# First stage of a graph network layer: x transposed loaded whole, bucket counts interleaved with the chunks of h

## The chip, the cores and the metric

The kernel runs on one core of one Trainium2 chip. The metric is device time in microseconds, the median of several runs. The core has TensorE (PE), VectorE (DVE), ScalarE (ACT), GpSimd (POOL) and SyncE (SP), which run on their own and wait for each other through semaphores, and 16 DMA engines that move what SP, ACT and POOL issue. SP's transfers go through one queue (q1 in the profile), ACT's through another (q10).

## What is computed

```python
h = x @ W_in2f                                        # x: 6250 x 128
Wij = ssp(f_ij @ W_filt1 + b_filt1) @ W_filt2 + b_filt2   # 200000 edges, 20 features
Wij = Wij * rcut_ij[:, None]
x_ij = h[idx_j] * Wij                                 # idx_j = dst, sorted
agg = segment_sum(x_ij, idx_i, num_segments=6250)     # idx_i = src, random
out = ssp(agg @ W_out1 + b_out1) @ W_out2 + b_out2
return layernorm(x + out)
```

`ssp` is softplus less log 2.

## The kernel before

Every engine has its program written out by hand; nothing is reordered by a scheduler. There are three parts.

**The first stage** (the subject here) computes h in 13 chunks of 512 nodes, the last of 256. For chunk n, PE multiplies the transposed x with `w_in` into `pre_psum[n % 2]` (`node_features`), ACT copies the high bf16 part to `h_out` (`h_hi`), DVE takes the rest (`h_left`), ACT its bf16 part (`h_mid`), DVE the last part (`h_lo`), and SP stores the three parts to `h_parts` in HBM (`store_h`). In front of each high part ACT also issues DMAs that fill four tables in HBM with zeros, 20 of 640 KB in all (`zero`). Both x and `h_out` have two buffers: SP loads x chunk by chunk (`load_x_t`), and ACT waits until the store two chunks back has landed. Chunks 0 and 1 stand alone, 2 to 11 in a loop of two per turn.

The first stage also prepares indices. DVE reduces `dst_g` (102 partitions of 2048 values) to window bases that go to HBM and come back (`window_base`, `base_all`), and casts `dst_g` and `src_g` to 16 bits, which SP stores (`dst`, `src`, semaphore `edges16_stored`) and reads back as broadcasts (`dst_b`, `src_b`). One fourth of the edge groups is routed by a table of 14 buckets of nodes: after chunk 1, `place_routed` on DVE marks which edge lies in which bucket (`in_bucket`), PE counts with four matmuls per bucket (`count_in_buckets`), and DVE multiplies each count with its mark and adds it to `rank`. `judge_windows` then sets the flag `narrow`, on which all engines branch, and `make_biases` splits the biases.

**The main loop** takes 391 groups of 512 edges. Of the groups that aren't routed, POOL adds the rows to the tables with indirect DMAs of 128 rows each (`scatter`, line 729), 1115 in all. Its order on each engine is a fixed list (`unit`). **The last layers** read the tables and write the output.

SP and POOL run their queues in order too: a wait holds back every transfer issued behind it.

Of the kernel before, what the change touches and what calls it, by code (L numbers as in the profile page):

```python
# [61 lines left out]
META_HOTS, META_STEPS = 20, 49  # L62
# [223 lines left out]
def build(nc, t):  # L286
    with ExitStack() as ctx:
# [75 lines left out]
        acc_t = sb("acc_t", [P, NODE_ROWS], F32)  # L363
# [16 lines left out]
        x_t = at(37632, "x_t", [P, 2, CHUNK], F32)  # L380
        h_out = at(41728, "h_out", [P, 2, 4, 3, DIM], BF16)
        h_rest = at(47872, "h_rest", [P, 2, 4, DIM], F32)
        bucket = at(51968, "bucket", [P, ROUTES * TILES], F32)
        local = at(53760, "local", [P, ROUTES * TILES], F32)
        src_r = at(55552, "src_r", [P, ROUTES * TILES], I32)
        in_bucket = at(58496, "in_bucket", [P, BUCKETS, ROUTES * TILES], BF16)
        rank = at(71040, "rank", [P, ROUTES * TILES], F32)
        rank_part = at(72832, "rank_part", [P, ROUTES * TILES], F32)
        bias_tmp = at(74880, "bias_tmp", [P, 2, 3, DIM], F32)
        bias_hi = at(77952, "bias_hi", [P, 2, 3, DIM], BF16)  # L390
        base_all = at(79488, "base_all", [P, SLOTS], F32)
        spread_row = at(81120, "spread_row", [1, SLOTS], F32)
# [30 lines left out]
        zeros_made, tables_zeroed = sem("zeros_made"), sem("tables_zeroed")  # L423
# [34 lines left out]
        meta_step, meta_mm, crowd_mm = sem("meta_step"), sem("meta_mm"), sem("crowd_mm")  # L458
# [28 lines left out]
        def run_chunks(eng, step, last):  # L487
            step((0, 0), CHUNK // P)
            step((0, 1), CHUNK // P)
            with eng.Fori(0, FULL_CHUNKS // 2 - 1) as j:  # L490
                step((j, 2), CHUNK // P)
                step((j, 3), CHUNK // P)
            step((0, FULL_CHUNKS), last // P)
# [281 lines left out]
        def _(act):  # L775
# [14 lines left out]
            for fifth in range(2):  # L790
                zero(0, fifth)
# [1365 lines left out]
```

## Time and profile before

| | us |
|---|---|
| median of 3 runs (lowest, highest) | 2372.86 (2367.43, 2375.89) |
| the profiled execution | 2375.85 |
| its span, from the first to the last instruction | 2373.8 |
| busy in the span: PE / DVE / ACT / POOL | 2162.8 / 1676.7 / 1642.3 / 1828.8 |
| last chunk of h split by DVE | 111.1 |
| first matmul of the main loop | 111.9 |
| first scatter / last scatter ends its chain | 128.3 / 2276.4 |

The span is read as three lengths: up to the first scatter, the scatters, and what is behind them. Matmul and DMA times are those of this one execution. TensorE runs at one of two clocks, and a row of windows gives the mean that was granted as a share of the full one.

### The profile page before, as it was taken

The page shows a single profiled execution, that of the slowest core. Times are in us where ns is not written, and L with a number is a line of the kernel's source. Part 1 is how long each engine was busy: PE and PEld are TensorE (multiplying, and loading weights), DVE is VectorE, ACT ScalarE, POOL GpSimd, SP SyncE. Part 2 cuts the span into 40 slices and gives each one's busy share as a digit, 9 for nine tenths or more (in the row PEclk, how much of TensorE's full clock was granted, in tenths as well). Part 3 has the DMA queues.
Part 4 walks back from the last instruction along what each step waited for, and adds up shares of the span by engine and source line. Part 5 has one row for each costly group of instructions (what it writes and reads, how often), then busy time and mean ns, then how long its engine had stood idle before and what let it go on. Part 6 is the DMA issues. An engine that isn't in the chain of part 4 may idle for free.

```text
span 2373.8 us, 60910 instructions
## 1 busy us (share of the span) xinstructions
PE 2162.8 (91%) x16558; PEld 1441.8 (61%) x16558; DVE 1676.7 (71%) x3915; ACT 1642.3 (69%) x3676; POOL 1828.8 (77%) x1148
## 2 busy tenths in 40 slices
PE   2488999999999999999999999999999999999947
PEld 1355666666656666666666666666666666666536
DVE  5466777777777777777776777777676768777627
ACT  0277777777777777777776877777776867777513
POOL 2068888888888888888888888888888888888831
PEclk8599999999999999999999999999999999999979
DMA  6676666666656666666666666666666656666555
GB/s 207 265 151 95 97 95 91 100 99 90 97 95 94 97 96 97 93 94 99 93 95 94 100 90 100 95 96 92 96 97 89 101 94 98 91 97 99 58 122 164
DMA packets 370946, 250.03 MB, mean 105 GB/s; under 512 B 88787, under 2 KB 350142, under 8 KB 370314
## 3 DMA queue, kind: packets, MB, share of 16 engines
q0 software_dynamic: 160560, 73.14, 32.6%
q1 hardware_dynamic: 199482, 155.27, 27.2%
q10 hardware_dynamic: 10476, 16.77, 1.9%
q8 instruction: 164, 2.69, 0.5%
q14 instruction: 264, 2.16, 0.4%
HBM read 149.90 MB, written 95.13 MB: 103 GB/s over the span
## 4 chain that ended last, share of the span: by engine, by line
DMA 44%; POOL 18%; PE 17%; issue 16%; DVE 3%; ACT 1%; POOLq 0%; SPq 0%; DVEq 0%; ACTq 0%
DMA table<-total,index 41%; POOL table L729 18%; PE unit_psum L1859 4%; PE unit_psum L1878 3%; PE both_psum L1815 2%; PE total_psum L1828 2%; PE pre_psum L1802 2%; DMA src_g<-in_src 1%; DMA h_parts<-h_out 1%; PE both_psum L2086 1%; PE both_psum L1840 1%; PE both_psum L1811 1%; PE both_psum L2084 0%; PE total_psum L2108 0%; PE pre_psum L2094 0%
## 5 line engine op out<-in xcount | busy, mean ns | idle before, releaser
L729 POOL DMA_INDIRECT table<-total,index x1115 | 1801.1, 1615 | 445.1 <-issue 244.6
L1859 PE MATMUL unit_psum<-moving,route_hot 128*128 128x386 bf16 x3136 | 608.1, 331 | 40.3 <-ACT ring L909 34.6
L879 ACT ACTIVATE h_dst<-both_psum,cols 128x128 f32<-128x128 f32 x1564 | 448.8, 385 | 104.2 <-PE both_psum L1840 104.2
L1878 PE MATMUL unit_psum<-scat_hot,ring 64*128 64x448 bf16 x4704 | 478.7, 351 | 9.6 <-DVE scat_hot L1416 6.1
L1859 PEld LDWEIGHTS unit_psum<-moving,route_hot 128*128 128x128 bf16 x3136 | 295.8, 99 | 267.5 <-ACT ring L909 103.6
L909 ACT ACTIVATE ring<-unit_psum 128x386 bf16<-128x386 f32 x784 | 373.2, 508 | 120.5 <-PE unit_psum L1859 82.0
L1815 PEld LDWEIGHTS both_psum<-w_f,hidden 128*128 128x128 f32 x3128 | 418.0, 194 | 18.3
L1815 PE MATMUL both_psum<-w_f,hidden 128*128 128x128 f32 x3128 | 418.8, 277 | 0.0
L1878 PEld LDWEIGHTS unit_psum<-scat_hot,ring 64*128 64x128 bf16 x4704 | 216.0, 94 | 216.9 <-DVE acc_t L1432 7.4
L1828 PE MATMUL total_psum<-message,same 128*128 128x129 f32 x2232 | 310.1, 281 | 4.0 <-DVE message L1344 2.4
L843 ACT ACTIVATE soft<-pre_psum 128x1024 f32<-128x1024 f32 x196 | 201.8, 1030 | 160.9 <-PE pre_psum L1802 159.8
L1828 PEld LDWEIGHTS total_psum<-message,same 128*128 128x128 f32 x2232 | 277.6, 192 | 36.5 <-issue 26.1
L862 ACT ACTIVATE total<-total_psum 128x516 f32<-128x516 f32 x279 | 171.2, 614 | 146.5 <-DMA table<-total,index 137.4
L1392 DVE TENSOR_SCALAR route_hot<-node_iota,cols 128x896 bf16<-128x896 uint16 x448 | 193.0, 477 | 98.8 <-PE unit_psum L1859 98.0
L1416 DVE TENSOR_SCALAR scat_hot<-node_iota,slot_node 128x448 bf16<-128x448 uint16 x784 | 255.9, 353 | 4.3 <-PE unit_psum L1878 2.5
L1297 DVE TENSOR_TENSOR same<-src_b,cols 128x512 f32<-128x512 uint16 x279 | 191.3, 686 | 93.7 <-PE total_psum L1828 92.7
L1318 DVE SCALAR_TENSOR_TENSOR hidden<-pre_psum,soft 128x1024 f32<-128x1024 f32 x196 | 238.9, 1219 | 21.0 <-ACT soft L855 19.6
L1344 DVE TENSOR_TENSOR message<-both_psum,h_dst 128x512 f32<-128x512 f32 x279 | 191.1, 685 | 84.3 <-ACT h_dst L879 37.0
L1802 PE MATMUL pre_psum<-f_t,w_f 32*128 32x512 f32 x784 | 224.7, 649 | 15.2 <-DVE hidden L1318 10.8
L849 ACT ACTIVATE soft<-soft 128x1024 f32<-128x1024 f32 x196 | 212.6, 1085 | 0.0
L855 ACT ACTIVATE soft<-soft 128x1024 f32<-128x1024 f32 x196 | 210.6, 1075 | 1.1
L1308 DVE TENSOR_SCALAR pick<-dst_b,cols 128x512 bf16<-128x512 uint16 x391 | 149.7, 383 | 85.5 <-PE both_psum L1840 65.9
(116 smaller groups left out, 1635.6 us busy)
## 6 DMA issues: line engine op xcount, KB each, us to landing
dst_b<-dst SPq DMA_DIRECT2D x391, 128.0 KB
src_b<-src SPq DMA_DIRECT2D x279, 128.0 KB, 4.3
f_t<-in_f_t SPq DMA_DIRECT2D x98, 256.0 KB
table<-total,index POOLq DMA_INDIRECT x1115
table<-zeros ACTq DMA_DIRECT2D x20, 640.0 KB, 5.6
window<-h_parts SPq DMA_DIRECT2D x391, 32.0 KB
parts<-table SPq DMA_DIRECT2D x48, 256.0 KB, 4.0
h_parts<-h_out SPq DMA_DIRECT2D x12, 384.0 KB, 5.4
```

The source lines that it names most:

```text
L729: pool.indirect_dma_start(tables[table], bass.IndirectOffsetOnAxis(index[:, i, k:k + 1], 0), total[:, i, k, 0:DIM], None, compute_op=ALU.a ...
L849: act.activation(soft[:, :, :], soft[:, :, :], ACT.Exp, scale=-1.0).then_inc(exp_done, 1)
L855: act.activation(soft[:, :, :], soft[:, :, :], ACT.Ln, bias=1.0).then_inc(soft_done, 1)
L879: last = act.activation(h_dst[:, b, d], source, ACT.Copy, scale=cols[:, g[1] // HALF % 2, weight:weight + 1])
L909: act.activation(ring[:, r[1] % RING, k, :], unit_psum[:, k % 2, 0:MOVING], ACT.Copy).then_inc(ring_done, 1)
L1318: dve.scalar_tensor_tensor(hidden[:, first:first + 2, :], pre_psum[:, :, :], 0.0, soft[:, :, :], ALU.max, ALU.add).then_inc(hidden_done, 1)
L1416: dve.tensor_scalar(scat_hot[:, r[1] % RING, :], node_iota[:, 0:BUCKET], slot_node[:, r[1] % RING, k:k + 1], None, ALU.is_equal).then_inc( ...
L1802: last = pe.matmul(pre_psum[:, a, :], w_f1[row:row + BAND, :], f_t[row:row + BAND, quad[1] % 2, :], start=True, stop=True)
L1815: last = pe.matmul(filter_psum[:, d], hidden[:, g[1] % QUAD, k * P:(k + 1) * P], w_f2[:, :], start=False, stop=(k == TILES - 1))
L1828: last = pe.matmul(total_psum[:, k // 2, d], same[:, b, k, :], message[:, b, k, :], start=True, stop=True)
L1859: last = pe.matmul(unit_psum[:, k % 2, 0:MOVING], route_hot[:, tile, k * P:(k + 1) * P], moving[:, tile, :], start=(tile == 0), stop=(tile ...
L1878: last = pe.matmul(unit_psum[:, strip, 0:BUCKET], ring[rows, r[1] % RING, slot_tile(m), part * DIM:(part + 1) * DIM], scat_hot[rows, r[1] ...
```

## The change

- **x**: `x_t` lies whole in the space of `acc_t` (the accumulator that POOL clears later). SP loads it in three parts (4, 4 and 5 chunks, `X_PARTS`), the first right behind `dst_g`, the others behind `src_g`; `src_i` and `weight_c` now come last.
- **h**: four buffers of `h_out` (`H_BUFFERS`); ACT waits for the store four chunks back. The loop is unrolled. SP issues no loads of x between the stores, and its first loads for the main loop (`load_first_edges`: features, `dst_b`, `src_b`) stand behind the store of chunk 6, not ahead of the stores.
- **counts**: DVE does `make_order` and the marks (`place_routed`) ahead of chunk 0. PE counts bucket n behind the matmuls of chunk n (bucket 13 last), and DVE multiplies with the mark between its two halves of chunk n (`take_ranks`), into two buffers of `rank_part`.
- **ranks**: the 13 additions are done by POOL, which does the cast of `src_g` first. POOL clears `acc_t` behind them, since x lies there.
- **tail**: `place_slots`, `judge_windows` and `make_biases` stand behind the last chunk; the bias matmuls too. PE's first matmul needs only `w_in`, and not all constants.
- **zeros**: ACT issues them between its two copies of a chunk, one table after another (`ZEROS_BY_CHUNK`: 2, 2, 2, 2, 1, 2, 1, 2, 1, 2, 1, 1, 1), and the first scatter of each table waits for that table alone.

```diff
+H_BUFFERS = 4
+X_PARTS = (0, 4, 8, 13)
+ZEROS_BY_CHUNK = (0, 2, 4, 6, 8, 9, 11, 12, 14, 15, 17, 18, 19, 20)
...
+            load_x_t(0)
             sp.dma_start(src_r[:, :], t["src_routed"]).then_inc(src_routed_loaded, 16)
-            sp.dma_start(src_i[:, :], t["src_cols"]).then_inc(src_cols_loaded, 16)
-            load_x_t((0, 0), CHUNK // P)
-            load_x_t((0, 1), CHUNK // P)
-            sp.dma_start(weight_c[:, :], t["weight_cols"]).then_inc(cols_loaded, 16)
             sp.dma_start(src_g[:, :, :], t["src"].rearrange("(p g e) -> p g e", p=QUADS, e=GROUP)
                          ).then_inc(src_loaded, 16)
+            load_x_t(1)
+            load_x_t(2)
+            sp.dma_start(src_i[:, :], t["src_cols"]).then_inc(src_cols_loaded, 16)
+            sp.dma_start(weight_c[:, :], t["weight_cols"]).then_inc(cols_loaded, 16)
...
+            def store_chunk(c, tiles):
+                store_h(c, tiles)
+                if is_at(c, CHUNKS // 2):
+                    load_first_edges()
+
+            run_chunks(store_chunk)
...
+            pool.wait_ge(src_loaded, 16)
+            pool.tensor_copy(src_g16[:, :], src_g[:, :, :].rearrange("p g e -> p (g e)")).then_inc(src16_made, 1)
             pool.wait_ge(src_cols_loaded, 16)
             pool.tensor_copy(edge_cols[:, :, 0:WEIGHT_COL], by_half(src_i[:, :])).then_inc(cols_made, 1)
             pool.wait_ge(cols_loaded, 16)
             pool.tensor_copy(edge_cols[:, :, WEIGHT_COL:WINDOW_COL], by_half(weight_c[:, :])).then_inc(cols_made, 1)
+
+            for b in range(1, BUCKETS):
+                pool.wait_ge(rank_taken, b + 1)
+                if b > 1:
+                    pool.wait_ge(rank_summed, b - 1)
+                pool.tensor_tensor(rank[:, :], rank[:, :], rank_part[:, b % 2, :], ALU.add).then_inc(rank_summed, 1)
+            pool.wait_ge(h_mm, CHUNKS)
             pool.memset(acc_t[:, :], 0.0).then_inc(acc_zeroed, 1)
...
             def split_h(c, tiles):
-                b = c[1] % 2
...
+                b, out = c[1] % 2, c[1] % H_BUFFERS
                 act.wait_ge(h_mm, after_chunk(c))
-                previous(act, h_stored[b], c, landed_chunk)
...
+                if c[1] >= H_BUFFERS:
+                    act.wait_ge(h_stored[out], 16 * (c[1] // H_BUFFERS))
...
+                for n in range(ZEROS_BY_CHUNK[c[1]], min(ZEROS_BY_CHUNK[c[1] + 1], FIFTHS * TABLES)):
+                    zero(n // FIFTHS, n % FIFTHS)
                 act.wait_ge(h_left, after_chunk(c))
...
+            def take_ranks(b):
+
+                dve.wait_ge(count_mm, b + 1)
+                dve.wait_ge(bucket_hot, BUCKETS)
+                if b >= 3:
+                    dve.wait_ge(rank_summed, b - 2)
+                part = rank[:, :] if b == 0 else rank_part[:, b % 2, :]
+                dve.tensor_tensor(part, unit_psum[:, b % 2, 0:ROUTES * TILES], in_bucket[:, b, :], ALU.mult
+                                  ).then_inc(rank_taken, 1)
...
+            make_order()
+            place_routed()
+            run_chunks(split_h)
+            for b in range(CHUNKS, BUCKETS):
+                take_ranks(b)
+            place_slots()
+            judge_windows()
+            make_biases()
```

On VectorE, behind chunk 1 of h, the program before has its marks, then 14 products and 13 additions in a row (the first of them here; `h_rest` and `h_out` are the two halves of a chunk):

```order
L1276 TENSOR_TENSOR h_out<-h_rest,h_out 128x4x128 [waits h_left,h_mid]
L1202 TENSOR_SCALAR rank_part<-src_r 128x448 [waits consts_made,src_routed_loaded]
L1205 TENSOR_SCALAR rank<-rank_part 128x448 [waits meta_step]
L1207 TENSOR_SCALAR bucket<-rank 128x448 [waits meta_step]
...
L1228 TENSOR_TENSOR rank<-unit_psum,in_bucket 128x448 [waits meta_step,meta_mm]
L1228 TENSOR_TENSOR rank_part<-unit_psum,in_bucket 128x448 [waits meta_step,meta_mm]
L1233 TENSOR_TENSOR rank<-rank,rank_part 128x448 [waits meta_step]
```

With the change the same engine has the marks ahead of chunk 0, and one product inside each chunk (here the end of the marks and chunks 0 and 3):

```order
L1225 CAST local_parts<-local 128x448 [waits local_step]
L1227 TENSOR_TENSOR local_parts<-local,local_parts 128x448 [waits local_step]
L1278 TENSOR_TENSOR h_rest<-pre_psum,h_out 128x512 [waits h_hi]
L1237 TENSOR_TENSOR rank<-unit_psum,in_bucket 128x448 [waits bucket_hot,count_mm]
L1284 TENSOR_TENSOR h_out<-h_rest,h_out 128x4x128 [waits h_left,h_mid]
...
L1278 TENSOR_TENSOR h_rest<-pre_psum,h_out 128x512 [waits h_lo,h_mid,h_hi]
L1237 TENSOR_TENSOR rank_part<-unit_psum,in_bucket 128x448 [waits rank_summed,bucket_hot,count_mm]
L1284 TENSOR_TENSOR h_out<-h_rest,h_out 128x4x128 [waits h_left,h_mid]
```

The additions are gone from VectorE, and each product from the fourth on waits for one of GpSimd's additions (`rank_summed`).

SyncE's queue with the change, from its start to the flag (`x_t` is x transposed, `h_parts` the stores):

```order
L544 DMA dst_g<-in_dst 102x2048
L535 DMA x_t<-in_x_t 128x2048
L547 DMA src_r<-in_src_routed 128x448
L548 DMA src_g<-in_src 102x2048
L535 DMA x_t<-in_x_t 128x2048
L535 DMA x_t<-in_x_t 128x2304
L552 DMA src_i<-in_src_cols 128x1632
L553 DMA weight_c<-in_weight_cols 128x1632
L556 DMA window_base<-dst_low 102x4 [waits spans_made]
L557 DMA window_spread<-dst_spread 102x4
L560 DMA dst<-dst_g_56 102x2048 [waits dst16_made]
L562 DMA src<-src_g_57 102x2048 [waits src16_made]
```

```order
L564 DMA base_all<-window_base 128x408 [waits spans_stored]
L565 DMA spread_row<-window_spread 1x408
L539 DMA h_parts<-h_out 128x1536 [waits h_lo] x7
L571 DMA f_t<-in_f_t 128x512 x2
L576 DMA dst_b<-dst 128x512 [waits edges16_stored]
...
L539 DMA h_parts<-h_out 128x1536 [waits h_lo] x5
L539 DMA h_parts<-h_out 128x768 [waits h_lo]
```

All of x, `src_i` and `weight_c` now stand ahead of the small store of the windows, and every store of h stands behind the wait for that store to land (`spans_stored`). Before, only 512 KB of x and the same columns stood there, and the loop of stores came last too.

## Rows read from the trace of the kernel before

**Rows 1.** Windows by stage: busy us (instructions) of each engine, TensorE clock, DMA share.

```profile
core 0: us, PE busy (x) PEld busy (x) DVE busy (x) ACT busy (x) POOL busy (x), PEclk, DMA share, GB/s
...
49.00:72.00 23.00, 12.16 (x55) 7.08 (x54) 20.92 (x48) 0.72 (x2) 0.00 (x0) 0.84 0.25 79
72.00:110.00 38.00, 19.00 (x68) 16.39 (x68) 13.33 (x20) 11.90 (x20) 0.00 (x0) 0.50 0.98 381
...
128.30:2276.40 2148.10, 2037.95 (x15884) 1346.33 (x15883) 1560.05 (x3605) 1585.99 (x3568) 1801.14 (x1115) 0.99 0.63 95
```

**Rows 2.** Timeline from 110 to 130 us: start, us, engine, line.

```profile
110.69 0.43 DVE L1276 TENSOR_TENSOR h_out<-h_rest,h_out 128x256 bf16<-128x256 f32 x1 [0.48 <-ACT h_out L808]
...
111.90 2.08 PE L1802 MATMUL pre_psum<-f_t,w_f 32*128 32x512 f32 x4 [3.91 <-issue]
...
128.34 1.73 POOL L729 DMA_INDIRECT table<-total,index  x1 [100.16 <-DVE index L1363]
```

**Rows 3.** DMA answer for 22 to 26 us, packets and busy share by queue.

```profile
DMA packets 98, 0.48 MB, mean 120 GB/s; under 512 B 33, under 2 KB 33, under 8 KB 50
...
q1 hardware_dynamic: 48, 0.39, 31.2%
```

**Rows 4.** DMA answer for 76 to 110 us, packets and landing times.

```profile
DMA packets 4092, 13.37 MB, mean 393 GB/s; under 512 B 448, under 2 KB 576, under 8 KB 4092
...
table<-zeros ACTq DMA_DIRECT2D x11, 640.0 KB, 4.6
h_parts<-h_out SPq DMA_DIRECT2D x8, 384.0 KB, 5.3
```

**Rows 5.** DMA issues from 0 to 130 us, KB of each, two sizes.

```profile
dst_g<-in_dst SPq DMA_DIRECT2D x1, 816.0 KB
...
dst<-dst_g SPq DMA_DIRECT2D x1, 408.0 KB
```

**Rows 6.** Timeline of the first 44 us, VectorE and SyncE's queue.

```profile
14.80 2.29 DVE L1144 TENSOR_REDUCE dst_low<-dst_g 102x4 f32<-102x2048 int32 x1 [14.80 <-DMA dst_g<-in_dst]
...
29.69 1.23 DVE L1151 CAST src_g<-src_g 102x2048 uint16<-102x2048 int32 x1 [9.00 <-DMA src_g<-in_src]
...
34.06 0.35 SPq L555 DMA_DIRECT2D base_all<-window_base  x1
...
35.57 0.39 DVE L1202 TENSOR_SCALAR rank_part<-src_r 128x448 f32<-128x448 int32 x1
...
42.18 0.66 DVE L1220 TENSOR_TENSOR local_parts<-local,local_parts 128x448 bf16<-128x448 f32 x1
...
43.64 0.33 SPq L567 DMA_DIRECT2D dst_b<-dst  x1
```

**Rows 7.** Groups of instructions from 43 to 72 us, counts and ranks.

```profile
L1767 PE MATMUL unit_psum<-in_bucket,ones_bias 128*128 128x336 bf16 (+2 forms) x42 | 10.4, 367 | 0.0
...
L1233 DVE TENSOR_TENSOR rank<-rank,rank_part 128x448 f32<-128x448 f32 x13 | 8.1, 624 | 0.4
L1765 PE MATMUL unit_psum<-in_bucket,earlier 128*128 128x448 bf16 x14 | 6.5, 466 | 15.7 <-DVE local_parts L1220 11.3 <-DVE rank_part L1228 4.3
```

**Rows 8.** Groups of instructions from 72 to 111.5 us, chunks of h.

```profile
L1780 PE MATMUL pre_psum<-w_in,x_t 128*128 128x128 f32 x68 | 19.1, 460 | 19.7 <-DMA x_t<-in_x_t 17.0 <-DVE h_rest L1271 2.7
...
L1276 DVE TENSOR_TENSOR h_out<-h_rest,h_out 128x512 bf16<-128x512 f32 (+1 forms) x11 | 7.3, 668 | 7.4 <-ACT h_out L808 7.4
...
L804 ACT ACTIVATE h_out<-pre_psum 128x512 bf16<-128x512 f32 (+1 forms) x10 | 5.8, 576 | 18.2 <-DMA h_parts<-h_out 18.2
```

**Rows 9.** Groups by form, GpSimd's only addition.

```profile
L769 POOL TENSOR_TENSOR half_sum<-parts 128x512 f32<-128x512 f32 x12 | 15.2, 1265 | 58.6 <-DMA parts<-table 58.6
```

**Rows 10.** Timeline of VectorE behind the last rank addition, and biases.

```profile
62.67 0.62 DVE L1233 TENSOR_TENSOR rank<-rank,rank_part 128x448 f32<-128x448 f32 x1
...
70.21 0.91 DVE L1194 COPY bias_o<-bias_hi 1x512 bf16<-1x512 bf16 x3
```

**Rows 11.** Timeline at 35 us, one issue on ScalarE's queue.

```profile
34.97 1.58 ACTq L783 DMA_DIRECT2D table<-zeros  x1
```

More of the change, by code:

```diff
@@ L485, in run_units, with run_chunks @@
             rest()
[L487 to L493, printed above, removed]
+        def run_chunks(step):
+            for n in range(CHUNKS):
+                step((0, n), (LAST_H if n == CHUNKS - 1 else CHUNK) // P)
         def run_last_layers(eng, step):
@@ L506, in previous, with h_landed @@
                 eng.wait_ge(s, count(plus(c, -n)))
+        def h_landed(eng):
+            for b in range(H_BUFFERS):
+                eng.wait_ge(h_stored[b], 16 * len(range(b, CHUNKS, H_BUFFERS)))
         def done_with(eng, s, g, kind=every, n=0):
@@ L624, in step_narrow @@
                 if is_at(g, 1):
-                    for k in range(2):
-                        sp.wait_ge(h_stored[k], 16 * (FULL_CHUNKS // 2 + (k == 0)))
+                    h_landed(sp)
                     load_window((0, 0))
@@ L758, in _ @@
                 pool.wait_ge(cols_made, 2)
-                for b in range(2):
-                    pool.wait_ge(h_stored[b], 16 * (FULL_CHUNKS // 2 + (b == 0)))
+                h_landed(pool)
                 run_groups(pool, step_general)
@@ new lines, in make_biases, with count_in_bucket @@
+            def make_biases():
+                pe.wait_ge(consts_loaded, 16 * 7)
+                pe.matmul(total_psum[:, 0, 0:DIM], minus_ln2[:, :], w_f2[:, :], start=True, stop=True)
+                pe.matmul(total_psum[:, 0, DIM:2 * DIM], minus_ln2[:, :], w_o2[:, :], start=True, stop=True
+                          ).then_inc(bias_mm, 1)
+            def count_in_bucket(b):
+                counts = unit_psum[:, b % 2, 0:ROUTES * TILES].rearrange("p (g k) -> p g k", k=TILES)
+                here = in_bucket[:, b, :].rearrange("p (g k) -> p g k", k=TILES)
+                pe.wait_ge(bucket_hot, b + 1)
+                if b >= 2:
+                    pe.wait_ge(rank_taken, b - 1)
+                pe.matmul(counts, earlier[:, :], here, start=True, stop=False)
+                for a in range(1, TILES):
+                    last = pe.matmul(counts[:, :, a:TILES], ones_bias[:, :], here[:, :, 0:TILES - a],
+                                     start=False, stop=(a == TILES - 1))
+                last.then_inc(count_mm, 1)
```

237 lines of the change are left out of this document (98 added, 139 removed).

## The prediction

> **What bounds the kernel now.** I read the windows by stage first, to see which part of the span the change can touch. From 128.3 to 2276.4 us GpSimd issues all 1115 scatters, 2148.1/1115 = 1.93 us each, with TensorE busy 2038 of the 2148 us [rows 1]. The diff leaves the instructions of this part as they are, and each waits only for others of the same part, so it keeps its length and moves as a whole. What counts is the start. The timeline gives it: VectorE ends the last chunk at 110.69 + 0.43 = 111.1, the first matmul of the main loop begins at 111.9, the first scatter at 128.34 [rows 2], 16.4 us after that matmul. The work between these two is unchanged as well.
>
> So the question is when the first stage ends. Its windows show two halves that don't overlap. From 49 to 72 us VectorE is busy 20.9 of 23 us with counts, flag and biases, and the DMA engines 25%. From 72 to 110 us the DMA engines are busy 98% at 381 GB/s and VectorE 13.3 of 38 us [rows 1]. There ScalarE waited 18.2 us for stores of h to land [rows 8], TensorE 17.0 us for x. The first half wastes the DMA engines, the second is bound by them: laying them over each other is what this change can gain, and DMA time is what limits it.
>
> **How fast the DMA engines are.** From 76 to 110 us they moved 393 GB/s [rows 4]; over 16 engines that is 24.6 GB/s, 24 KB (of 1024) per us and engine. They don't share evenly: between 22 and 26 us, when only `src_g` was left on SP's queue, that queue kept 31% of 16 = 5 engines busy [rows 3]. `src_g` has 102 partitions, 6 x 17, so I take it that such a transfer lies on six engines, 816/6 = 136 KB on each [rows 5]. The trace doesn't name the six. The Trainium skill does (DMA: Bandwidth & Descriptors, "Why a DMA increments its semaphore by 16 and not by 1"): the largest count up to 16 that divides the slowest dimension, and always the lowest-numbered engines; the 31% agrees. By it all four such transfers pile up on the same six; spread over all 16, the transfers of the sum below would be done 170/24 = 7 us earlier.
>
> On one of the six, behind `dst_g`, there are on SP's queue: x 200, `src_r` 14, `src_g` 136, `src_i` and `weight_c` 51 each, `dst` and `src` 408/6 = 68 each, `base_all` 13, the stores of h 12 x 24 + 12 = 300, and the first edges 2 x 16 + 7 x 8 = 88: 989 KB. ScalarE's queue adds 20 x 40 = 800 KB of zeros. At 24 KB/us these 1789 KB take 74.5 us.
>
> **Part by part.**
> *Start.* `dst_g` is first on SP as before, and the constants are the same, so it lands at 14.8 [rows 6]. Its two reductions and the cast end at 20.7. VectorE then no longer waits for `src_g` (it did until 29.69), but does `make_order` (0.9 us) and the marks, which took 35.57 to 42.84, 7.3 us [rows 6]: chunk 0 begins on VectorE at 28.9. TensorE and ScalarE have their part of it by 20, since the first quarter of x lands 64/24 = 2.7 us behind `dst_g`.
>
> *Engines per chunk.* TensorE: 19.1/8.5 = 2.25 us for h [rows 8] and (10.4 + 6.5)/14 = 1.21 us for a count [rows 7], both mostly at its lower clock (0.50 granted in that window), 3.5 us. VectorE: 0.67 + 0.62 + 0.67 and handoffs, 2.2 us [rows 7, 8]. GpSimd: its addition of 512 columns took 1.265 us [rows 9], so 1.11 us for 448; hidden under the chunk. ScalarE: two copies of 0.6 us and the zeros' issue, up to 1.58 us each [rows 11], 2.8 to 4.4 us. None of this is the bound if the next step holds.
>
> *The stall.* Chunk 4 waits for store 0 to land. Store 0 is issued only when the small store of the windows has landed, which stands behind all of x and both columns. Ahead of its landing are on the six engines x 200, 14, 136, 102, 136, 13 and its own 24: 625 KB, and the zeros of chunks 0 to 3, 8 x 40 = 320 KB. 945/24 = 39.4 us from 14.8 gives 54.2. The small store itself, rows of 16 bytes, held SP from `src_g`'s landing at 29.69 to 34.06 [rows 6], 4.4 us; half of that overlaps with zeros, so 2 more: 56. The way of counting, tried on before: from 34.06 the two 16-bit stores (136 KB) and three tables of zeros (120) in front of `dst_b`'s issue at 43.64 [rows 6] take 10.7 us; the trace has 9.6. The other waits are shorter: GpSimd starts its additions behind `weight_c` (about 43), and VectorE's product 3 waits for one of them, but both end before 56.
>
> *From 56 on* the two queues share: 12 KB/us for SP. Chunk 11 needs store 7, behind stores 1 to 7 (168 KB) and the first edges (88): 256/12 = 21 us, 77. TensorE alone would bring chunk 11 at 56 + 6 x 3.5 = 77 too, being two chunks ahead. Chunk 12 follows at 79, and VectorE ends it at T = 81. The last store lands at 86, all zeros by about 90: both before they are needed.
>
> *The tail.* What lay under nothing before lies under nothing now: product 13 (0.62), GpSimd's addition (1.11), handoffs 0.2, then the same work as from 63.3 to 71.1, 7.8 us [rows 10]; then TensorE reads the flag and starts, 1.6 us (0.8 behind VectorE's last instruction before [rows 2], and that one it didn't wait for). 11.3 us in all: first matmul at 92.3 instead of 111.9. Clearing `acc_t` on GpSimd (5.3 us) moves behind the additions and fits under the 16.4 us.
>
> *Zeros by table.* The first scatter at 108.7 finds all zeros landed, as it did before: 0.
>
> Sum: -19.6 us. Span 2373.8 - 19.6 = 2354.2; the profiled execution took 2375.85, 3 us above the median of 2372.86, which becomes 2353.
>
> *A rule that speaks against it.* No row has VectorE and GpSimd adding from SBUF at once. The Trainium skill (SBUF — State Buffer, "Who interferes with whom") says that a VectorE instruction with two SBUF inputs and a GpSimd one that reads SBUF exclude each other. By it each chunk's second half could wait one addition: 3.3 us of VectorE per chunk, below TensorE's 3.5, and the total would be about 2354.
>
> **Rivals.**
> *A. The engines are the bound, the DMA engines are not* (15%). If the zeros take less of the six engines than half, store 0 lands before chunk 4 asks. Then 11 chunks at TensorE's 3.5 us from 29.6 and the last split end at 70, first matmul 81.5, total 2342. For it: a 64 KB share that lands in 3 us when its queue has the engines. Against: 98% busy with fewer zeros per us than now.
> *B. The old pace from chunk 4 on* (14%). From 72 to 110 a chunk took about 4.2 us; 56 + 9 x 4.2 = 94, first matmul 105, total 2366. For it: stores took 5.3 us to land [rows 4], and queue depth might count, not bytes. Against: x is no longer in that queue.
> *C. The shift is lost in the main loop* (6%): total 2370 to 2373. GpSimd is idle 347 us in it [rows 1], so a lost start could be made up there; but TensorE, at 95%, starts later too.
> *D. Slower* (5%). The small store in front of all stores of h: its 16-byte rows alternate with zeros on the same engines. If it lands so late that store 0 comes after 75.6 (then T passes 100.6 and the first matmul 111.9), the kernel is slower; at 81 by 5 us, 2378. It took 4.4 us before with at most one table beside it, and would need some 20.
>
> **How the numbers follow.** The likeliest case, DMA-bound with the stall at 56, has 60%; its own range is 2346 to 2361, by store 0 at 50 to 62. The range for 8 in 10 runs from A to B, 2341 to 2367. 0.3% is 7 us, about what this measurement can tell, as its own runs lie 8 us apart. Faster by more than that: the likeliest, A and half of B, 0.83; within it: the rest of B and C, 0.12; slower: 0.05.
>
> **What would show it.** First matmul of the main loop at 90 to 95, first scatter 16 behind. ScalarE idle some 10 us ahead of chunk 4's high part, released by a store of `h_parts`; SP's queue held at `base_all` to 43 or later. DMA share above 0.8 from 30 to 86. Main loop unchanged at 2148. Wrong: chunk 4 before 50 (A), chunks 8 to 12 apart by 4 us (B), a longer main loop (C), `base_all` after 60 (D).

## The result, and the profile after

| | before | after |
|---|---|---|
| median of 4 (lowest, highest) | 2374.27 (2367.43, 2375.89) | 2409.68 (2407.33, 2415.37) |
| ratio, 95% interval | | 1.0152 (1.0135 to 1.017) |
| span of the profiled execution | 2373.8 | 2413.3 |
| first matmul of the main loop | 111.9 | 104.46 |
| first scatter | 128.34 | 121.72 |
| from the first scatter to the end of the last one's chain | 2148.1 | 2189.0 |
| behind that | 97.4 | 102.6 |

The change made the kernel 1.5% slower. The start moved forward as forecast in sign (6.6 us, not 19.6), the main loop became 40.9 us longer, and 5.2 us were lost behind it: -6.6 + 40.9 + 5.2 = 39.5 us, the difference of the spans. Of the 5.2 no cause was found, and it may be none: the part behind the last scatter took between 96 and 103 us in kernels of both kinds (96.5 in `a_pad62` below, 101.7 in `b_pad34`, which has the old first stage).

**The first stage after.** Windows of the changed kernel, columns as in [rows 1]; the last row is the part from the first scatter on.

```profile
0.00:30.00 30.00, 8.81 (x33) 6.92 (x34) 16.32 (x33) 3.00 (x4) 5.55 (x18) 0.99 0.94 252
30.00:56.40 26.40, 9.13 (x40) 7.18 (x38) 6.03 (x10) 2.87 (x6) 6.71 (x5) 0.63 0.70 277
56.40:84.90 28.50, 17.80 (x80) 14.68 (x80) 19.17 (x21) 8.03 (x15) 7.92 (x7) 0.80 0.99 375
84.90:104.50 19.60, 2.38 (x12) 1.53 (x12) 16.46 (x35) 2.22 (x5) 8.80 (x4) 0.50 0.31 122
121.70:2310.70 2189.00, 2051.70 (x15883) 1356.50 (x15880) 1559.84 (x3605) 1586.55 (x3567) 1786.52 (x1115) 0.97 0.61 94
```

Overlap came about: the DMA engines are busy 94, 70 and 99% up to 84.9, where before they were at 25% from 49 to 72 [rows 1]. Then come 19.6 us at 31%. The timeline shows what lies at the seams (L815 is the start of a chunk on ScalarE, here chunks 4 and 11; L1284 the last part of chunk 11).

```profile
46.23 0.36 SPq L564 DMA_DIRECT2D base_all<-window_base  x1
...
56.39 0.60 ACT L815 ACTIVATE h_out<-pre_psum 128x512 bf16<-128x512 f32 x1 [21.06 <-DMA h_parts<-h_out]
...
66.19 2.49 SPq L571 DMA_DIRECT2D f_t<-in_f_t  x2
...
78.19 11.92 SPq L539 DMA_DIRECT2D h_parts<-h_out  x6
...
84.89 0.60 ACT L815 ACTIVATE h_out<-pre_psum 128x512 bf16<-128x512 f32 x1 [9.17 <-DMA h_parts<-h_out]
...
86.82 1.13 POOL L726 TENSOR_TENSOR rank<-rank,rank_part 128x448 f32<-128x448 f32 x1 [10.02 <-DVE rank_part L1237]
...
86.91 1.59 DVE L1284 TENSOR_TENSOR h_out<-h_rest,h_out 128x512 bf16<-128x512 f32 x1 [0.17 <-ACT h_out L821]
...
91.94 5.32 POOL L728 MEMSET acc_t<- 128x6272 f32 x1
...
93.47 4.01 DVE L1260 TENSOR_SCALAR edge_cols<-base_all,row_node 128x408 f32<-128x408 f32 x1
...
104.46 2.08 PE L1817 MATMUL pre_psum<-f_t,w_f 32*128 32x512 f32 x4 [11.38 <-issue]
...
121.72 1.73 POOL L747 DMA_INDIRECT table<-total,index  x1 [24.45 <-issue]
```

Chunk 4 starts on ScalarE at 56.39, behind a wait of 21 us for store 0 (forecast: 56, behind some 10 us). From 66.19 to 78.19 SyncE issues the first edges, 12 us for nine transfers; the stores of h stand behind them, and ScalarE waits 9.2 us for store 7 ahead of chunk 11: 84.89, forecast 77. The last part of h is done at 89.75, forecast 81. Beside GpSimd's addition (86.82) the last part of a chunk (L1284) takes 1.59 us. The clearing of `acc_t` at 91.94 lies over `judge_windows`, whose 128x408 operation takes 4.01 us. First matmul 104.46, forecast 92.3.

**The main loop after.** TensorE's waits from 128 to 2300 us (line, what it waited for, us in total, times, longest), changed kernel and then the one before:

```profile
PE both_psum L1830 <- issue: 48.8, 13, 4.6
PE both_psum L1826 <- issue: 29.3, 13, 2.5
PE unit_psum L1874 <- ACT ring L922: 20.6, 25, 3.1
```

```profile
PE unit_psum L1859 <- ACT ring L909: 34.6, 41, 3.3
...
PE both_psum L1811 <- issue: 33.1, 13, 3.8
```

The loop has 13 turns. Each kernel loses 2.3 to 2.5 us per turn in "issue", a wait for nothing that the profile shows, ahead of the first matmul of a turn. The changed one has a second such wait per turn, in the midst of the matmuls of L1830: 48.8 us. The turn at 636 us, after and before:

```profile
635.61 0.39 PE L1826 MATMUL both_psum<-bias_f,ones_bias 96*128 96x512 bf16 x1 [2.04 <-issue]
635.84 0.72 PE L1830 MATMUL both_psum<-w_f,hidden 128*128 128x128 f32 x5
640.87 1.01 PE L1830 MATMUL both_psum<-w_f,hidden 128*128 128x128 f32 x3 [4.31 <-issue]
641.67 2.78 PE L1874 MATMUL unit_psum<-moving,route_hot 128*128 128x386 bf16 x8
```

```profile
636.08 0.39 PE L1811 MATMUL both_psum<-bias_f,ones_bias 96*128 96x512 bf16 x1 [2.27 <-issue]
636.31 1.06 PE L1815 MATMUL both_psum<-w_f,hidden 128*128 128x128 f32 x8
637.20 1.48 PE L1859 MATMUL unit_psum<-moving,route_hot 128*128 128x386 bf16 x8
```

Eight matmuls of one line run as one before; now three of them start 4.31 us later. And what follows runs slower, 2.78 us for the eight matmuls that took 1.48. The windows of the changed kernel from the gap on show the clock:

```profile
635.70:640.80 5.10, 0.86 (x6) 0.64 (x6) 0.00 (x0) 2.38 (x6) 4.19 (x4) 0.60 0.79 139
640.80:650.00 9.20, 9.13 (x52) 6.46 (x54) 4.39 (x8) 4.34 (x11) 7.79 (x5) 0.67 0.51 70
```

TensorE did 0.86 us of work in 5.1, and the granted clock falls to 0.60 and 0.67, a mix of the 1.2 and the 2.4 GHz level; the kernel before has 1.00 there. So the balance of the loop is +48.8 for the second stall, -3.8 at the first, -14.0 at the waits for the ring (ScalarE can catch up meanwhile), +13.8 of busy time (2051.7 against [rows 1]). That is 44.8 us; by difference the waits not listed are some 4 us shorter, which leaves the 40.9.

### The profile page after: what moved, and what is told of

The parts are those of the page before. It is cut to its first block, busy times and chain, and to the rows that moved or that the text cites. A ratio compares the mean times of both kernels' runs of the same rounds, so it can differ in the third digit from the quotient of the medians.

```text
span 2413.3 us, 60781 instructions
## 1 busy us (share of the span) xinstructions
PE 2177.6 (90%) x16558; PEld 1455.5 (60%) x16558; DVE 1678.5 (70%) x3901; ACT 1642.3 (68%) x3676; POOL 1831.1 (76%) x1162
## 4 chain that ended last, share of the span: by engine, by line
PE 36%; DMA 31%; issue 15%; POOL 11%; DVE 3%; ACT 2%; SPq 1%; POOLq 0%; DVEq 0%; ACTq 0%
DMA table<-total,index 28%; POOL table L747 10%; PE unit_psum L1874 9%; PE unit_psum L1893 8%; PE both_psum L1830 6%; PE total_psum L1843 5%; PE pre_psum L1817 4%; PE both_psum L1855 2%; PE both_psum L1826 1%; DMA window_spread<-dst_spread 1%; ACT ring L922 1%; PE both_psum L2101 1%; DMA h_parts<-h_out 1%; ACT h_dst L892 1%; DMA parts<-table 1%
## 5 line engine op out<-in xcount | busy, mean ns | idle before, releaser
L1874 PE MATMUL unit_psum<-moving,route_hot 128*128 128x386 bf16 x3136 | 617.4, 335 | 22.7 <-ACT ring L922 20.6
L1830 PE MATMUL both_psum<-w_f,hidden 128*128 128x128 f32 x3128 | 422.9, 278 | 48.8 <-issue 48.8
L1830 PEld LDWEIGHTS both_psum<-w_f,hidden 128*128 128x128 f32 x3128 | 418.6, 194 | 69.8 <-issue 51.5
L1843 PE MATMUL total_psum<-message,same 128*128 128x129 f32 x2232 | 315.0, 284 | 4.2 <-DVE message L1355 2.7
L1843 PEld LDWEIGHTS total_psum<-message,same 128*128 128x128 f32 x2232 | 282.8, 195 | 36.0 <-issue 24.6
L875 ACT ACTIVATE total<-total_psum 128x516 f32<-128x516 f32 x279 | 171.8, 616 | 112.3 <-DMA table<-total,index 99.8
L1817 PE MATMUL pre_psum<-f_t,w_f 32*128 32x512 f32 x784 | 224.7, 649 | 21.9 <-issue 11.4
```

The source lines that it names most:

```text
L1817: last = pe.matmul(pre_psum[:, a, :], w_f1[row:row + BAND, :], f_t[row:row + BAND, quad[1] % 2, :], start=True, stop=True)
L1830: last = pe.matmul(filter_psum[:, d], hidden[:, g[1] % QUAD, k * P:(k + 1) * P], w_f2[:, :], start=False, stop=(k == TILES - 1))
L1843: last = pe.matmul(total_psum[:, k // 2, d], same[:, b, k, :], message[:, b, k, :], start=True, stop=True)
L1874: last = pe.matmul(unit_psum[:, k % 2, 0:MOVING], route_hot[:, tile, k * P:(k + 1) * P], moving[:, tile, :], start=(tile == 0), stop=(tile ...
```

## The experiments

All times are medians of 4 to 10 runs. The ratios are against runs of the kernel before taken beside each kernel: their median was 2374.3 for the changed kernel, 2375.3 for `b_pad66` and the three that begin with a, 2374.4 for `b_pad34` and those with c, 2377.7 for those with d. "First matmul" and "scatters" (from the start of the first to the start of the last scatter) are of one profiled execution each, which lies up to 7.3 us from the median of its kernel. Positions count the instructions of TensorE's program as built (a bf16 matmul with its weight load is 2, a float32 one 4).

| kernel | loop starts at | median | ratio to before (95%) | first matmul | scatters |
|---|---|---|---|---|---|
| before | 3889 | 2374.3 | | 111.9 | 2144.6 |
| after | 4021 | 2409.7 | 1.0152 (1.0135, 1.0170) | 104.5 | 2185.6 |
| b_pad34 | 3956 | 2372.4 | 0.9996 (0.9979, 1.0012) | 109.3 | 2140.7 |
| b_pad66 | 4020 | 2412.8 | 1.0153 (1.0133, 1.0172) | 108.3 | 2183.4 |
| a_pad12 | 4045 | 2374.6 | 0.9995 (0.9981, 1.0008) | 104.9 | 2148.8 |
| a_pad62 | 4145 | 2371.4 | 0.9987 (0.9973, 1.0001) | 104.5 | 2140.2 |
| c_memset_late | 4145 | 2369.7 | 0.9981 (0.9965, 0.9998) | 106.0 | 2145.7 |
| a_pad62_dve | 4145 | 2364.0 | 0.9957 (0.9941, 0.9973) | 99.4 | 2148.9 |
| d_stores_first | 4145 | 2364.0 | 0.9948 (0.9927, 0.9969) | 99.8 | 2141.7 |
| d_biases | 4145 | 2360.8 | 0.9944 (0.9922, 0.9967) | 96.0 | 2142.7 |
| c_edges_last | 4145 | 2358.6 | 0.9929 (0.9908, 0.9950) | 89.8 | 2153.1 |
| c_zeros_late | 4145 | 2355.4 | 0.9928 (0.9907, 0.9950) | 90.7 | 2144.5 |
| d_all_edges6 | 4145 | 2352.5 | 0.9891 (0.9858, 0.9923) | 85.2 | 2146.0 |
| d_all | 4145 | 2349.2 | 0.9880 (0.9843, 0.9917) | 82.1 | 2143.4 |

### Where the loop lies in TensorE's program

The diff puts 132 instructions more ahead of TensorE's loop, by unrolling the chunks; the loop itself, 2211 instructions, is the same. Theory F: the second stall depends on where the loop starts. Rival: something that the new first stage leaves behind (table zeros, buffers, the order of queues) slows the loop. The edit is small matmuls into a corner of PSUM that isn't in use yet ahead of TensorE's first real one, 62 and 12 of them in the changed kernel, 66 in the kernel before:

```diff
+            pe.wait_ge(consts_made, CONSTS)
+            for _ in range(62):
+                pe.matmul(both_psum[0:1, 0, 0:1], ones_bias[:, 0:1], ones_bias[:, 0:1], start=True, stop=True)
             pe.wait_ge(w_in_loaded, 16)
-            pe.wait_ge(consts_made, CONSTS)
```

`a_pad62`, expected:

> The changed kernel with 62 one-element matmuls on TensorE ahead of its first real one (124 instructions with their weight loads), where it waits for x anyway. Theory F, place in the code: the change moved the start of TensorE's main loop by +132 instructions, so that a block of code ends about 14 instructions behind the loop's start and every turn waits 3.8 us for the next block; 124 more make the shift 256, a multiple of 128 and of 256, and the second stall (48.8 us over 13 turns at line 1830's matmuls) is gone: span about 2413 - 45 to 50 = 2363 to 2368, main loop 2140 to 2150, clock 0.99. Theory G, data traffic or the new places of buffers slow the loop: nothing changes, 2410 +- 5, main loop 2187.

`b_pad66`, expected:

> The kernel before with 66 one-element matmuls on TensorE (132 instructions) while it waits for its constants, nothing else changed: the loop starts within one instruction of where the changed kernel has it. F: a second stall of 3 to 4.5 us in each of 13 turns appears and the time is 2373 + 40 to 55 = 2413 to 2428, though the first stage is the old one. G: 2373 +- 5.

`a_pad12`, expected:

> The changed kernel with 12 such matmuls (24 instructions): the loop starts some 10 instructions behind the end of a block, with nearly a whole block ahead of it. F: as with 62, the second stall is gone, 2363 to 2368; if the distance mattered otherwise, the stall moves elsewhere in the turn. G: 2410.

Measured: 124 instructions more make the changed kernel 38 us faster, and 131 more make the kernel before 37 to 38 us slower. The medians lie 3 to 7 us above the 2363 to 2368 that was expected of `a_pad62` and `a_pad12`, and that of `b_pad66` just under its 2413 to 2428; theory G, with 2405 or more for the first two and 2378 or less for the third, is far off. TensorE's waits of `a_pad62`, then of `b_pad66`:

```profile
PE unit_psum L1876 <- ACT ring L922: 39.2, 46, 2.9
...
PE both_psum L1828 <- issue: 30.8, 13, 3.7
```

```profile
PE both_psum L1817 <- issue: 46.4, 13, 4.2
PE both_psum L1813 <- issue: 30.1, 13, 2.9
```

`a_pad62` has no second stall, `b_pad66` has it at the same matmuls as the changed kernel (L1817 is its L1830), with the old first stage. The rival is out. `a_pad12`, 24 instructions on, is free of it too (29.4 us at the first stall alone).

The stall falls behind the 14th instruction of a turn in the changed kernel (two of loop control, one bf16 matmul, five of the eight records of four float32 ones: 2 + 2 + 10) and behind the 16th in `b_pad66` (six of eight), that is, at 4035 to 4036 of the program in both. `a_pad12`, which starts past it, doesn't stall. So something ends there, and a turn that starts 14 or 16 instructions ahead of it stalls. How far ahead is enough? `b_pad34` starts 79 ahead:

> Kernel before with 34 one-element bf16 matmuls ahead of TensorE's first real one: its loop starts at instruction 3956 of its program (before: 3889, where a turn has one stall for code; 4020: two). If the second stall comes because the loop starts only some 14 instructions ahead of the end of a block of 256 that is fetched as one, 79 are enough: one stall per turn of 2.2 to 2.8 us, and the median within 0.3% of before, 2368 to 2380. Rival: what counts is the length of the code ahead (every added instruction slows), or the distance needed is over 79: a second stall per turn, median 2390 to 2415.

```profile
PE both_psum L1813 <- issue: 32.2, 13, 3.2
```

One stall per turn, 2372.4 us. The Trainium skill (Runtime: NRT & Kernel Launch, "Instruction fetch mechanics") says that an engine's code is fetched in 16 KiB blocks of 256 instructions, one after the other, and that a jump to a block outside the current window of two forces a fetch before the engine goes on. The trace agrees: the instruction queue q8 moves packets of 16.4 KB, and every kernel stalls once per turn, at the jump.

The packets also stand in the traces with their times (`--dma` with a narrow window). In the turn at 636 us one lands at 634.07, and the first matmul of the turn starts at 635.61; the next lands at 639.46, and the second stall ends at 640.87. So it is in all 13 turns of the changed kernel and of `b_pad66`: a packet lands 1.5 to 1.9 us ahead of the end of the first stall, and another 1.2 to 1.6 us ahead of the end of the second. Kernels without the second stall have two such packets as well. There the second lands 2.2 to 4.8 us after the turn's first matmul, and TensorE works meanwhile. So the next block arrives 2 to 5 us into the turn wherever the loop lies; with 14 to 16 instructions left in the first one the engine has run dry, with 79 it hasn't (0.7 us of such waits in all of `b_pad34`). Nothing in the trace names the engine that a packet of q8 belongs to; that these are TensorE's is inferred from their place, at 26 of 26 second stalls. The count alone doesn't tell the kernels apart (174 in the changed kernel, and 174 in `b_pad34`, which doesn't stall twice).

### GpSimd beside VectorE

In `a_pad62` the first stage still ends 12 us later than forecast. Part of it is the tail, 14.9 us there (14.7 in the changed kernel) from the last part of h to the first matmul instead of 11.3. `a_pad62_dve` gives the 13 rank additions back to VectorE, behind each product:

```diff
+                    dve.tensor_tensor(rank[:, :], rank[:, :], rank_part[:, b % 2, :], ALU.add).then_inc(rank_summed, 1)
```

> As with 62, and the 13 additions of ranks on VectorE again, right behind each product. Theory L: an addition on GpSimd and a VectorE instruction with two inputs in SBUF exclude each other (h_out took 1.60 instead of 0.69 us beside each addition). Undone, a chunk costs VectorE 2.0 + 0.65 instead of 2.9 us, and the tail loses GpSimd's addition but keeps one of 0.62: 1 to 3 us faster than with 62. Rival: VectorE doesn't set the pace of the chunks (the stores do), so equal to the run with 62 within 2 us.

```profile
73.49 5.33 POOL L723 MEMSET acc_t<- 128x6272 f32 x1 [32.74 <-PE pre_psum L1785]
...
84.36 0.60 ACT L810 ACTIVATE h_out<-pre_psum 128x512 bf16<-128x512 f32 x1 [11.30 <-DMA h_parts<-h_out]
...
92.00 0.40 DVE L1258 TENSOR_SCALAR edge_cols<-base_all,row_node 128x408 f32<-128x408 f32 x1
...
99.38 2.08 PE L1817 MATMUL pre_psum<-f_t,w_f 32*128 32x512 f32 x4 [7.77 <-issue]
```

VectorE does 0.63 us more per chunk, and a chunk goes from 2.9 us down to 2.4, since L1282 takes 0.69 us again and not 1.59. At the end of h that gives only 0.3 us (89.3 against 89.6), since store 7 holds chunk 11 as before. The rest, more than expected, came in the tail, 10.0 us: with no additions ahead of it, the clearing moves to 73.49 and the 128x408 operation takes 0.40 us instead of 4.01. First matmul 99.4, 5.1 us earlier; median 7.4 us lower. Is it the clearing? `c_memset_late` leaves the additions on GpSimd and clears behind the flag:

```diff
             pool.wait_ge(h_mm, CHUNKS)
-            pool.memset(acc_t[:, :], 0.0).then_inc(acc_zeroed, 1)
-
             pool.wait_ge(flag_made, 1)
+            pool.memset(acc_t[:, :], 0.0).then_inc(acc_zeroed, 1)
```

> Base: the changed kernel with 62 small matmuls ahead of TensorE's program (2371.4 us; rank additions on GpSimd; first matmul at 104.5). Only difference: GpSimd clears acc_t behind the flag and not ahead of it. Theory M (the clearing holds VectorE's operations while it runs: the 128x408 subtraction took 4.0 us beside it): that operation takes 0.4 us, the tail from the last part of h to the first matmul falls from 14.7 to 10 to 11.5 us, and the first matmul comes at 100 to 101.5; the wait then falls on VectorE's operations at the start of the main loop instead, of which one takes 3 us or more beside the clearing, so that the median falls by 0 to 3 us. Rival N (the 4.0 us are the late landing of base_all or a queue of SBUF writes): the operation stays at 4 us, the tail at 14 to 15.

```profile
93.82 0.40 DVE L1259 TENSOR_SCALAR edge_cols<-base_all,row_node 128x408 f32<-128x408 f32 x1
...
95.50 5.32 POOL L729 MEMSET acc_t<- 128x6272 f32 x1 [3.16 <-DVE narrow L1269]
...
95.84 5.13 DVE L1191 CAST bias_hi<-bias_tmp 128x256 bf16<-128x256 f32 x1
```

The 128x408 operation is free (0.40 us), and the cast of 128x256, 0.29 us by itself, starts 0.34 us after the clearing and ends with it: 5.13 us. The tail gained nothing (15.9 us), so half of the expectation failed (first matmul 106.0, not 100 to 101.5), and for the very reason that theory M names: the collision moved on to the next such instruction, ahead of the first matmul and not behind it. The landing of `base_all` (rival N) is out. The median, 1.6 us below that of `a_pad62`, is within the scatter of both.

Not every instruction is held by it. In `c_edges_last`, below, the clearing runs from 74.61 to 79.94 and L1282, which reads two operands of SBUF, takes 0.68 us in its midst. The Trainium skill (SBUF — State Buffer, "Who interferes with whom") has both: two SBUF inputs collide with a GpSimd instruction that reads SBUF, not with one that only writes; casts and `tensor_scalar`, in their fast modes, with either. Which mode an instruction took isn't in the trace, but the durations agree on each: the last part of a chunk beside an addition 1.59, beside the clearing 0.68; the scalar operation and the cast beside the clearing 4.01 and 5.13.

### What holds store 7

Theory S: SyncE's 12 us of issue. Theory T: the bandwidth, 99% busy from 56 to 85. Two edits on `a_pad62_dve`. `c_edges_last`:

```diff
-                if is_at(c, CHUNKS // 2):
+                if is_at(c, CHUNKS - 1):
                     load_first_edges()
```

> Base: the changed kernel with 62 small matmuls ahead of TensorE's program and the rank additions on VectorE (2364.0 us; chunk 11 of h waits 11.3 us for store 7, first matmul of the main loop at 99.4). Only difference: SyncE's 9 first loads for the main loop are issued behind the store of chunk 12, not behind that of chunk 6. Theory S (the 12 us in which SyncE issues them hold back store 7): ScalarE's wait ahead of chunk 11 ends at 73 to 77 instead of 84.4, the last part of h is done at 79 to 83, and first_edges then take some 4 us of issue and land by 90; the first matmul comes at 91 to 95 and the median falls by 4 to 8 us. Rival T (the transfer bandwidth is the bound there, 370 GB/s and 97% busy from 56 to 85): the waits stay within 2 us of 84.4 and the median within 2 us, or is later because the edges now land later.

`c_zeros_late`, one zero transfer per chunk and seven behind the last:

```diff
-ZEROS_BY_CHUNK = (0, 2, 4, 6, 8, 9, 11, 12, 14, 15, 17, 18, 19, 20)
+ZEROS_BY_CHUNK = (0, 1, 2, 3, 4, 5, 6, 7, 8, 9, 10, 11, 12, 13)
```

> Same base. Only difference: one zero transfer per chunk of h, and the 7 that are left (4.6 MB) behind the last chunk. Theory T (bandwidth bound from 56 to 85): ahead of chunk 11 there are 5 to 6 zeros fewer, 3.5 MB or some 9 us at 390 GB/s, so ScalarE's wait ends 6 to 9 us earlier and the first matmul comes at 91 to 94; the first edges issue faster too. The median falls by 3 to 8 us unless the last tables' zeros (now landing at about 105 to 110) hold a scatter. Theory S: SyncE's issue of the first edges stays at 10 to 12 us and store 7 as late, within 2 us.

`c_edges_last` (chunk 11 on ScalarE is the second row), then `c_zeros_late`:

```profile
74.61 5.33 POOL L723 MEMSET acc_t<- 128x6272 f32 x1 [32.69 <-PE pre_psum L1785]
...
74.76 0.60 ACT L810 ACTIVATE h_out<-pre_psum 128x512 bf16<-128x512 f32 x1 [0.71 <-DMA h_parts<-h_out]
...
77.19 0.68 DVE L1282 TENSOR_TENSOR h_out<-h_rest,h_out 128x512 bf16<-128x512 f32 x1
...
80.13 3.58 SPq L571 DMA_DIRECT2D f_t<-in_f_t  x2
...
89.44 0.35 DVE L1317 TENSOR_SCALAR pick<-dst_b,cols 128x512 bf16<-128x512 uint16 x1 [0.71 <-DMA dst_b<-dst]
```

```profile
60.53 1.46 SPq L571 DMA_DIRECT2D f_t<-in_f_t  x2
...
75.02 0.60 ACT L810 ACTIVATE h_out<-pre_psum 128x512 bf16<-128x512 f32 x1 [6.31 <-DMA h_parts<-h_out]
```

Both theories get their gain: chunk 11 starts 9.6 us earlier without the edges in front, 9.3 us earlier with fewer zeros beside them; the first matmuls, 89.8 and 90.7, came a little ahead of the expected 91. But the second gain is made of two: in `c_zeros_late` chunk 4 already starts at 52.23 and not 55.98, 3.8 us earlier, and ahead of chunk 11 6.3 us of the 11.3 remain. In `c_zeros_late` SyncE's issue of the edges takes 60.53 to 68.07, 7.5 us instead of 12, against theory S, which had it at 10 to 12. A transfer's issue takes longer while much is queued: 0.43 us for one of 128 KB after the stores (as at 99.07 in `a_pad62_dve`), 0.8 to 1.7 us in the block at 66 to 78 in the changed kernel. Most likely, then, what holds store 7 is the bytes ahead of it, edges and zeros, on DMA engines that are busy all the time, and SyncE's long issue is how that shows. No run takes away the issue alone, so this share of it is argued, not shown. Without the edges in front store 7 costs 0.7 us; with fewer zeros it still costs 6.3. The chunks between follow at 2.4 us, in which VectorE is busy throughout, and in `c_zeros_late` TensorE too.

### Store 0, the biases, and all together

`d_stores_first` moves SyncE's wait for the window bases behind store 3:

```diff
+                if is_at(c, H_BUFFERS - 1):
+                    load_spans()
```

> Base: the changed kernel with 62 small matmuls ahead of TensorE's program and the rank additions on VectorE (2364.0 us; SyncE issues the stores of chunks 0 to 3 at 46.5, behind its wait for the window bases, though chunk 3 is done at 39; ScalarE idles until store 0 lands at 56 to 57). Only difference: that wait and the two loads behind it come after store 3. Theory W (the wait is the bound): store 0 is issued at 31 and lands at 47 to 52, and chunk 4 starts 4 to 9 us earlier. Theory S and T (what binds later is the queue in front of store 7: 97% busy from 56 to 85) say that chunk 11 gains less than that: its wait ends at 79 to 83 instead of 84.4, first matmul at 94 to 98, median 2 to 5 us lower. If the stores are the bound all along, the whole 5 to 9 us arrive at the first matmul.

```profile
30.41 11.58 SPq L539 DMA_DIRECT2D h_parts<-h_out  x4
...
56.35 0.60 ACT L813 ACTIVATE h_out<-pre_psum 128x512 bf16<-128x512 f32 x1 [19.91 <-DMA h_parts<-h_out]
```

Theory W fell. Store 0 is issued at 30.4 instead of 46.5 and lands at 56.35 instead of 55.98: issuing it sooner is worth nothing here. The bytes queued ahead of it are the same. The later gain that was expected failed with it: chunk 11 at 84.7, first matmul 99.8, and the median is that of `a_pad62_dve`.

`d_biases` moves the bias matmuls and VectorE's `make_biases` behind chunk 3, into its idle time:

> Same base. Only difference: the bias matmuls and VectorE's bias operations stand behind chunk 3, in VectorE's 18 us of idle time, and not behind the flag. They are 4.9 us of the 10.0 us between the last part of h and the first matmul (93.5 to 98.4 in that trace). Theory: the whole 4.9 us is on the path, the first matmul comes at 94 to 95.5, and the median falls by 4 to 5 us. Rival: the flag, its branch and the first loads behind it (windows, dst_b) are next and take the gain, the first matmul stays later than 97.

```profile
85.65 0.60 ACT L810 ACTIVATE h_out<-pre_psum 128x512 bf16<-128x512 f32 x1 [11.52 <-DMA h_parts<-h_out]
...
96.00 2.08 PE L1819 MATMUL pre_psum<-f_t,w_f 32*128 32x512 f32 x4 [3.10 <-issue]
```

Last part of h at 90.6 (chunk 11 came 1.3 us later here), first matmul 5.4 us behind it instead of 10.0: the tail gives the whole 4.7 us. Of it 3.4 arrive at the first matmul (96.0, expected 94 to 95.5) and 3.2 in the median.

`d_all` joins all four edits, `d_all_edges6` all but the one on the edges:

> Both edits above, and also the first edges behind store 12 and one zero transfer per chunk with 7 behind the last. Chunks then follow at 2.4 us from 47 to 52 on: last part of h at 69 to 74, tail 5 us, but the first edges are issued only at 70 to 74 and then take some 8 us to land, beside 7 zeros on ScalarE's queue. First matmul of the main loop at 80 to 85 against 99.4, median 2345 to 2351 us, ratio to before 0.988 to 0.991; the table additions end 14 to 18 us earlier than in the base unless the late zeros hold a scatter.

> As d_all, but the first edges stay behind store 6 as in the changed kernel. Theory S (their 12 us of issue hold store 7): chunk 11 waits again, some 3 to 6 us; against that the edges are there when the main loop starts. First matmul within 3 us of d_all's, median 2345 to 2353 us; if the edges' late landing is what bounds d_all, this one is faster.

```profile
51.02 0.60 ACT L813 ACTIVATE h_out<-pre_psum 128x512 bf16<-128x512 f32 x1 [14.41 <-DMA h_parts<-h_out]
...
87.12 0.35 DVE L1323 TENSOR_SCALAR pick<-dst_b,cols 128x512 bf16<-128x512 uint16 x1 [10.13 <-DMA dst_b<-dst]
```

```profile
52.00:70.00 18.00, 16.77 (x82) 14.74 (x83) 17.73 (x31) 8.96 (x16) 1.47 (x1) 0.89 1.01 408
70.00:87.00 17.00, 2.78 (x10) 0.75 (x8) 6.78 (x19) 3.44 (x6) 3.85 (x1) 0.59 1.02 390
```

`d_all` is the fastest, 2349.2 us, 1.2% below the kernel before and 2.5% below the changed one. With one zero transfer per chunk store 0 lands at 51.0 (50.7 in `d_all_edges6`), against 56.4 in `d_stores_first` and 52.2 in `c_zeros_late`, where it is issued late: fewer bytes ahead give 3.8 us by themselves, and the earlier issue 1.2 to 1.5 more in these single executions. From 52 to 87 the DMA engines are at 101 and 102% of their share, and what the main loop then waits for is `dst_b`, landed at 87.1: 10.1 us of VectorE's time. The first matmul (82.1) has waited for the features, issued late as well. It comes 29.8 us and the first scatter 26.9 us earlier than before; the median is 28.5 us lower than that of the runs of before beside it (2377.7): the shift carries through the main loop. In `d_all_edges6` chunk 11 waits 7.2 us for its store again (expected 3 to 6), and the first matmul comes at 85.2; but its first scatter is at 101.92, that of `d_all` at 101.47, and the medians are 3.3 us apart with runs that overlap (2350.8 to 2353.6, 2345.1 to 2354.8). Which place of the edges is better these runs don't tell.

## Why the prediction was wrong, step by step

**The step that failed** is "The diff leaves the instructions of this part as they are, and each waits only for others of the same part, so it keeps its length and moves as a whole". The instructions are the same and so are their waits, but not where they lie in TensorE's program. The runs put a price on it: 35 to 41 us, with either first stage. In place of "keeps its length" they showed a second wait for the next block of code in each of 13 turns, 48.8 us, and 13.8 us more of busy time at the lower clock. The kernel before has 33.1 us of "issue" at the top of its 13 turns; that wait was in its trace and does not occur in the prediction. This was not the only step. With the loop in a good place the changed kernel takes 2371.4 or 2374.6 us, and not 2353: of the 19.6 us forecast for the first stage, 12.2 were not there. None of the rivals had the loop's mechanism: C's loop that grows ended at no gain, and D's slower case was another one, whose wait (`base_all` at 46.23) was as forecast.

**The first stage**, forecast at 92.3, came at 104.46.
- *Start and stall*: right in time. Chunk 0 was at 26.9 on VectorE (28.9), `base_all` at 46.2 (43 or later), chunk 4 at 56.39 (56). That bytes more than the place in SyncE's order set the landing of store 0 is what `d_stores_first` and `c_zeros_late` show. How the sum of 945 KB was weighed is less sure, and 56 is in part luck: by it four zeros fewer are worth 160/24 = 6.7 us, and they gave 3.8; the DMA share from 30 to 56 was 0.70 and not above 0.8. That would suit transfers that lie on six engines of 16, but no view shows the six.
- *From 56 on*: mis-sized. "12 KB/us for SP" gave 77 for chunk 11; it was 84.89. The bytes and the bound were right, the even split of the two queues was not: from 56.4 to 84.9 the zeros' queue q10 had 58.7% of the DMA engines and SyncE's q1 39.9%, 4.10 MB in 28.5 us, which is 8.8 KB (of 1024) per us on each of 16, and 256/8.8 = 29.
- *Engines per chunk*: TensorE's 3.5 us, by which it "alone would bring chunk 11 at 77 too", were wrong. The counts of [rows 7] had run at a granted clock of 0.84 and not 0.50, and from 56.4 to 84.9 the clock was 0.80; chunks 8 to 10 of `c_zeros_late` follow at 2.45 us with TensorE busy throughout, at 1.00. The spacing was 2.9 us, with L1284 at 1.59. The rule weighed in the prediction holds, but its price was 0.9 us per chunk and its place not the bound there.
- *Tail*: 14.7 us instead of 11.3. "Clearing `acc_t` on GpSimd (5.3 us) moves behind the additions and fits under the 16.4 us" failed: it starts as soon as the additions end, beside `judge_windows`, and costs 3.6 us.
- 7.9 (store 7) + 0.9 (chunks 11 and 12) + 3.4 (tail) = 12.2 us: the difference.

With the loop in a good place the change makes no measurable difference: 3.9 and 0.6 us below the runs of before beside them, with intervals that reach from 6.4 us faster to 1.9 slower. The 7.4 us at the first matmul don't show in full, and where the rest goes is open. **Rival C** (the shift is lost in the main loop) is nonetheless not borne out as a mechanism: `d_all` keeps 28.5 us. The chances were added up a little wrong (0.60 + 0.15 + 0.07 is 0.82, not 0.83), which changes nothing.

## What to carry to other kernels

Code ahead of a long loop is not free of effect on it: read the waits for "issue" at the loop's top and the times of q8's packets beside them, and compare two kernels only with the loop at the same place in its engine's program; a few instructions ahead of it tell whether that is the difference. Moving an addition to an idle GpSimd can cost VectorE more than the addition, and a large clearing there should lie beside instructions that it lets pass, as it did the subtraction here. A store that lands late behind a saturated queue is moved by taking bytes from in front of it; issuing it sooner gave at most 1.5 us here.

## What the runs showed of the hardware

- A loop of 2211 TensorE instructions stalls 2.3 to 2.8 us at each jump; where a turn starts 14 or 16 instructions ahead of one point of the program it stalls once more, 3.6 to 3.75 us on the mean of 13 (46.4 and 48.8 us), with 79 ahead or 10 past it not.
- In both kernels that stall twice a packet of the instruction queue q8 lands 1.5 to 1.9 us ahead of the end of each first stall and 1.2 to 1.6 us ahead of the end of each second one.
- In the window of that stall and the one behind it (14 us) the granted clock was 0.60 and 0.67, where the kernel before has 1.00, and the matmuls there took 2.78 instead of 1.48 us for eight.
- A GpSimd clearing of 128x6272, 5.3 us, held a 128x256 cast for 5.13 us and a 128x408 scalar operation for 4.01, and let a 128x512 subtraction pass in 0.68.
- Issuing a transfer of 128 KB from SyncE took 0.43 us after the stores and 0.8 to 1.9 us behind seven or more of them at 97% DMA and above; with fewer zeros beside them it took 0.5 to 1.6 us, at 97% too, so the busy share alone doesn't set it.
- From 56.4 to 84.9 us ScalarE's queue (640 KB fills) had 58.7% of the DMA engines and SyncE's 39.9%.
